# Two half pieces instead of three in each turn of the first block of a Householder tridiagonalisation, in a fused graph-network kernel

## What is computed

```python
h = max(layernorm(x), 0); x = x + L0(h, adj)   # 8 Euler steps of a linear ODE
h = max(layernorm(x), 0); x = x + L1(h, adj)   # filter in the eigenbasis of the Laplacian
h = max(layernorm(x), 0); x = x + L2(h, adj)   # GCN with batch norms
h = max(layernorm(x), 0); x = x + L3(h, adj)   # GCN twice, then LSTMs over windows
```

```python
def euler_step(h, _):
    ax = jnp.einsum('nm,bmd->bnd', adj_mx, h)
    f = alph * 0.5 * (ax - h) + h @ w_eff - h + x0
    return (h + dt * f, None)
```

## Time and profile before

| | us |
|---|---|
| median of 3 runs | 3958.34 |
| lowest and highest run | 3941.43, 3967.08 |
| profiled execution, its own time | 3942.42 |
| its span, first to last instruction | 3940.4 |
| PE busy in it | 2820.6 (72%) |
| DVE busy in it | 2967.6 (75%) |
| ACT busy, Pool busy | 1013.3, 817.8 |

### The profile page before, as it was taken

One profiled execution on the slowest core, in us unless ns is written; L12 is line 12 of the kernel. 1 busy time (PEld: TensorE's weight loads), 2 busy tenths in 40 slices (PEclk: granted clock), 3 DMA queues, 4 the chain that ended last, 5 costly groups with the idle time before them and its releaser, 6 DMA issues.

```text
span 3940.4 us, 69222 instructions
## 1 busy us (share of the span) xinstructions
PE 2820.6 (72%) x20902; PEld 1912.1 (49%) x20902; DVE 2967.6 (75%) x18125; ACT 1013.3 (26%) x3729; POOL 817.8 (21%) x3348
## 2 busy tenths in 40 slices
PE   2899999888888989899996201122024199889999
PEld 1677777777777777555553101021011044344454
DVE  6777788888888887888888788899999922432454
ACT  0222222232232222222221100000001033534654
POOL 0122222222222222223332322332111000000110
PEclk7789999999999897999997555566567599989999
DMA  2000000000000000000000000000000000000001
GB/s 108 2 2 2 2 2 2 2 2 2 2 2 2 2 2 2 2 2 2 2 2 1 0 0 0 0 0 0 0 0 0 0 0 22 0 1 0 0 0 43
DMA packets 3687, 21.27 MB, mean 5 GB/s; under 512 B 496, under 2 KB 624, under 8 KB 2160
## 3 DMA queue, kind: packets, MB, share of 16 engines
q1 hardware_dynamic: 3312, 16.85, 1.1%
HBM read 12.66 MB, written 4.19 MB: 4 GB/s over the span
## 4 chain that ended last, share of the span: by engine, by line
DVE 47%; PE 35%; issue 6%; POOL 6%; ACT 4%; DMA 1%; DVEq 0%; POOLq 0%; SPq 0%; ACTq 0%
DVE H L2057 6%; PE ps L1104 4%; DVE jq L1631 4%; PE ps L746 3%; PE ps L738 3%; POOL step L1151 3%; PE ps L1111 3%; DVE H L1631 2%; POOL C L1152 2%; ACT sz L1406 2%; DVE PQ L1809 2%; PE ps L688 2%; DVE SO L1838 2%; DVE XYEG L1787 2%; ACT SO L1407 1%
## 5 line engine op out<-in xcount | busy, mean ns | idle before, releaser
L1151 POOL TENSOR_SCALAR step<-XYEG,PQ 128x8 f32<-128x8 f32 (+3 forms) x510 | 159.3, 312 | 1129.0 <-DVE PQ L1809 1129.0
L746 PE MATMUL ps<-C 128*32 128x131 f32 (+39 forms) x10200 | 375.3, 277 | 15.7 <-DVE C L1826 14.3
L1406 ACT ACTIVATE sz<-C,PQ 128x4 f32<-128x4 f32 (+3 forms) x510 | 151.5, 297 | 784.0 <-POOL C L1152 784.0
L738 PE MATMUL ps<-eye,same 128*128 128x384 f32 x766 | 342.1, 529 | 0.0
L1390 ACT ACTIVATE tsc<-tsc 128x1 f32<-128x1 f32 x510 | 103.5, 203 | 707.4 <-DVE tsc L1770 707.4
L746 PEld LDWEIGHTS ps<-C 128*32 128x32 f32 x10200 | 254.0, 114 | 53.6 <-DVE C L1826 19.6
L1631 DVE CUSTOM_DVE_ANT_0 jq<-SO,ps,C 128x10 f32<-128x10 f32 (+14 forms) x1199 | 220.1, 228 | 54.9 <-DVE SO L1838 2.0
L755 PEld LDWEIGHTS ps<-dots,C 128*128 128x128 f32 x1020 | 168.5, 198 | 186.5 <-DVE dots L1631 102.0
L768 PE MATMUL ps<-C,XYEG 128*128 128x2 f32 (+1 forms) x958 | 185.0, 269 | 101.2 <-POOL C L1152 98.9
L2057 DVE RECIPROCAL H<-H 128x8 f32<-128x8 f32 (+8 forms) x81 | 242.3, 2992 | 2.8
L768 PEld LDWEIGHTS ps<-C,XYEG 128*128 128x128 f32 x958 | 152.9, 196 | 184.7 <-POOL C L1152 183.4
(11 more groups left out here) (538 smaller groups left out, 7451.3 us busy)
## 6 DMA issues: line engine op xcount, KB each, us to landing
out_x<-X SPq DMA_DIRECT2D x8, 512.0 KB, 3.0
X<-in_x SPq DMA_DIRECT2D x2, 1280.0 KB, 20.7
X<-in_x SPq DMA_DIRECT2D x1, 1536.0 KB, 17.0
eye<-in_eye SPq DMA_DIRECT2D x1, 1026.0 KB, 9.4
WK<-in_adj SPq DMA_DIRECT2D x1, 1024.0 KB, 5.0
adjT<-in_adjT SPq DMA_DIRECT2D x1, 1024.0 KB, 7.0
WK<-in_below SPq DMA_DIRECT2D x1, 1024.0 KB, 11.2
V<-in_wih SPq DMA_DIRECT2D x1, 1024.0 KB, 4.8
```

The costliest lines, as they stand in the source:

```text
L738: mm(ps[:, 7, 0:n], ident, eye[:, 0, 0:n], start=True, stop=True)
L746: m = mm(ps[q * QUAD:(q + 1) * QUAD, 0, 0:c + n], SI[:, b, 0, 2 * j:2 * j + 1].broadcast_to([P, QUAD]), AS[:, b, q, k * QUAD:P + n], start ...
L1151: step(g_.tensor_scalar(step2[:, k:KB, :], this[:, :, 2:4], PQ[:, r % 2, 1:2], None, ALU.mult))
L1406: fn(sz[:, k:KB].unsqueeze(2), SI[:, k:KB, 0, 2 * j + 1:2 * j + 2], ACT.Copy, scale=PQ[:, r % 2, 2:3])
```

## The change

In block 0 a turn has room for two pieces instead of three. The rooms of the other blocks and of the panel updates are as they were.

```diff
-ROOM = ((3, 0), (3, 0), (3, 0), (2, 0))
+ROOM = ((2, 0), (3, 0), (3, 0), (2, 0))
```

## The result

| | us |
|---|---|
| after, median of 20 runs | 3972.43 (3956.96 to 3989.48) |
| before, 20 runs beside it | 3958.28 (3938.31 to 3968.67) |
| ratio after / before | 1.0037, 95% interval 1.0023 to 1.0051 |
| profiled execution after, its own time and span | 3957.96, 3956.1 |

A forecast was written before the change was run, and what follows sets the result against it. At full clock DVE's own chain bounds block 0's turns (3.85 to 4.2 us), row-matmul turns sticking out; the clock comes second. Terms -22 + 5 + 22 + 7 - 2 = +10 gave 3952, plus 16 to the median: 3968 us, range 3933 to 4018.

The forecast's parts named there:

- Relief in block 0: Block 0: without the third piece DVE's waits at line 1819 shrink, 15 us plus 7 in the table stage; -22 us.
- The w and L turns: Turns 28 to about 37: low clock with two pieces, ten turns 1.1 us too long against 6.4 us before; +5 us.
- the clock in the rest of block 0: Rest of block 0: two full pieces hold the clock less well, 20 further half-clock turns; +22 us.
- The sign that I had named: Block 0, 230 to 716 us: line 1770's wait for line 746 grows from 21.4 by 20 or more, clock below 0.90.
- the price of 1.1 us a turn: Block 0: a half-clock turn with two pieces takes 5.26 us against 4.10 at full clock.
- Block 1 unchanged: Block 1: only the order of pieces moves, so its length stays the same; 0 us.
- Work that moves into block 2: Block 2: stage ends 34 turns later, 33 filler turns get three pieces at 0.2 us a turn; +7 us.
- The tail: Stage end: two unfilled turns, 368 and 369, now start just behind a panel update instead of before one; -2 us.
- From the profile to the median: Whole kernel: median of three runs, 3958.34, lies 16 us above the profiled 3942.42; added to 3952, giving 3968.
- the clock sinks for much of block 0: Rival, chance 0.20: block 0 stays at low clock, 70 of 100 turns giving +65 us, 4023 us.
- the clock holds: Rival, chance 0.27: two pieces are work enough and w and L turns recover quickly; -19 us, 3939 us.

The follow-up runs named there:

- Experiment 12: Experiment 9's kernel with two pieces per turn in turns 1 to 27 only, three after; 3933.56 us, ratio 0.9977 to the kernel before.
- experiment 4: Kernel before without the row matmul (line 658) for all w tiles but the first; 3953.61 us, ratio 0.9968.
- the later execution: The changed kernel run once more, unedited, and profiled again; 3981.47 us, ratio 1.0035 to the kernel before.
- experiment 7: Kernel before with Pool's sixteen additions into X cut to one column of 128; 3945.97 us, ratio 0.9968.
- experiment 8: Changed kernel with Pool's additions into X cut to one column of 128; 3932.04 us, ratio 0.995 to the kernel before.
- experiment 3: Kernel before with the filler left out in turns 368 and 369 and the panel update ahead of 368; 3995.62 us, ratio 1.0078.
- experiment 5: Kernel before with fillers also in turns 334 and 335, and 512 instead of 384 filler columns in block 2; 3939.25 us, ratio 0.9964.
- experiment 9: Kernel before with w's row matmul moved to the turn's second pause, two empty turns filled, 512 filler columns in block 2; 3925.61 us, ratio 0.9898.
- experiment 1: Changed kernel with fillers also in turns 368 and 369 and the empty pauses of the panel update ahead; 3975.08 us, ratio 1.0023.

## Why the prediction came out as it did

*Relief in block 0* (-22). Right in kind and close in size: line 1819's wait fell by 23 us (35.8 to 12.6), and no w turn at full clock sticks out any more. The table stage gained 9.6 us, where 7 had been taken. Experiment 12 shows the table's part singly, and experiment 4 that the wait of the row matmul is worth 8 us in turns 28 to 128.

*The w and L turns and the clock in the rest of block 0* (+5, +22). Right in kind, too large by about 11 us. Turns 28 to 30 with w and L took 5.44 to 5.49 us at 0.50, where 5.26 was worked out, and the clock was back by turn 34 (267 us), not 37. Over turns 28 to 128 the two profiles of the changed kernel hold 8 and 12 half-clock turns against 4. The five profiles with two pieces in all of block 0 and whole additions take 474.1 to 488.2 us for this stretch, 481.5 in the mean; those of the unchanged kernel take 480.7 and 481.0. So relief and clock balance here, where +12 had been forecast. The sign that I had named, line 1770's wait up by 20 us or more, failed (21.4 to 23.6): half-clock turns also cost at line 1819 and in the panel updates, which the price of 1.1 us a turn left out: the one of turn 31 alone is 4.5 us longer. The granted clock of turns 28 to 128 is 0.91, not under 0.90; the later execution has 0.88.

*Block 1 unchanged* (0). Wrong, by +11.5 and +10.6 us. I had taken the order of pieces for neutral since their number is the same. The clock falls in other turns and more often: x0 and the turns behind it stay at half for nine turns in place of six, and seven turns of s1 and s0 join them. Additions are not it for the most part (experiments 7 and 8); why the clock falls at turns 133 and 195 and not elsewhere stays open.

*Work that moves into block 2* (+7). -6.1 in one profile and +6.9 in the other, about right with a spread that the sum didn't have. Turns 256 to 336 gain up to 14.8 us, presumably since the last group's s0 tiles and additions have left them; turns 336 to 368 lose 8.7 or more, except with small additions.

*The tail* (-2). This is the step that failed: +23.8 us. I priced it as two turns whose clock had already fallen, from the earlier trace rows, and took for granted that the filler runs at full clock, because in the one profile that I had the clock was back at once behind the stage. In the changed kernel it isn't until the next panel update, that of turn 383. And the gap is not two turns: "just behind a panel update" was read as a relief, while two of that update's pauses are empty as well, 11.4 us in all, and the low level begins in them. The profile before held the warning in another place: seven turns in a row at 0.52 with three pieces each. Why the clock takes so long to come back stays open.

*From the profile to the median* (+16). I carried the 16 us between profiled run and median over as an offset, with no cause. The cause that experiments 3 and 5 point to, never seen in a profile of the unchanged kernel, is the same fall behind turn 335, in part of the executions. On the chips of experiments 3 and 9, where it is usual, before is at 3971; on that of 5 it is at 3944. Beside the result itself two of before's 20 runs are at 3938 and 3941 and 18 at 3956 to 3969, a smaller gap than 25 us; what makes it smaller stays open. So before pays in some executions what the changed kernel pays in both of its profiles. The changed kernel's profile, too, is 14.5 us under its median (3957.96, the second lowest of 20), and that gap can't be this fall, which the profile already holds; the later profile is longer in turns 28 to 128 and 256 to 368 instead. So two offsets of 16 and 14.5 us with different content cancelled, and within the profiled +15.7 a term that was missing (+24) stood in for others that were too high. That the sum landed at 3968 for a measured 3972 is luck. *Rivals:* "the clock sinks for much of block 0" did not come, "the clock holds" neither; what happened is between them in block 0 and elsewhere in size.

## What to carry to other kernels

When filler matmuls are to hold a clock, ask apart whether they hold it and how soon they raise it again, and look at every place where useful work ends, pauses of special steps included: a gap of 11 us was followed by thirteen turns and more at half clock. When the profiled run is well under the median, find what the profile lacks before summing on it; sort the run times and look for groups. And before thinning out work to relieve one long turn, move the one instruction that sticks out behind the wait: it brought the relief here and kept the load.

## What the runs showed of the hardware

A stretch can stay at either level of the clock with the same instructions: thirteen turns with two fillers of 384 columns each at 1.00 (45.2 us, PE busy 39.96) and at 0.50 (66.2 us, PE busy throughout). Out of the low level the clock came back under such fillers after 17.1 us once (experiment 1), while in six stretches of five profiles it stayed low for thirteen turns or more, up to a panel update. With 512 columns the edited kernels' profiles had that stretch at 1.00 and no extra time, 45.2 us for the same thirteen turns. The clock also falls in turns with three pieces: over turns 352 to 367 of after it is 0.86 with PE busy 59.2 of 68.2 us. A stay at the low level behind turn 335 is the likely reason why run times of the unchanged kernel lie 25 us apart on one chip, and the share of each group differs from chip to chip (23 of 29 in the upper one, 11 of 35 on another).

Beside a Pool addition of 128 x 512 fp32 (1.26 us) a DVE instruction with several inputs takes 1.27 in place of 0.21 us; sixteen of them cost about 20 us (17 by this count, 21.6 between two profiled spans). The Trainium skill (GPSIMD Engine Reference, Specifications) names such contention for DVE instructions with two SBUF inputs, and the trace agrees.
